# State-space layer of a four-layer network: input and output statistics move from VectorE to ScalarE

## The reference, cut to what matters

```python
u = x.reshape(Bsz, C, H * W).transpose(0, 2, 1)
fx = _layernorm(u, ln1_g, ln1_b)                # over the 384 channels
Bu = jnp.einsum('ph,blh->blp', B_bar, fx)       # 192 complex states
_, xs = jax.lax.associative_scan(binop, (lam_el, Bu), axis=1)
y = 2.0 * jnp.real(jnp.einsum('hp,blp->blh', Cc, xs)) + D * fx
y = jax.nn.gelu(y, approximate=False) + fx
fy = _layernorm(y, ln2_g, ln2_b)
z1, z2 = jnp.split(fy @ W_enc.T, 2, axis=-1)
y = (z1 * jax.nn.gelu(z2, approximate=False)) @ W_dec.T + fy
```

## Time and profile before

| what | us |
|---|---|
| median of three runs (lowest to highest) | 4251.5 (4245.55 to 4254.65) |
| the profiled execution, its own time | 4248.17 |
| its span in the trace | 4246.4 |
| state-space layer: first group norm to its last output store issued | 1891.5 to 2651.6 |
| VectorE busy, whole span | 3092.6 (73%) |
| TensorE busy, whole span | 3846.9 (91%) |
| ScalarE busy, whole span | 2300.1 (54%) |

### The profile page before, as it was taken

How to read it: one execution, slowest core, us unless ns; L and a number is a source line. 1 busy time by engine, 2 the same in 40 slices (tenths; PEclk the granted TensorE clock), 3 DMA queues, 4 the chain that set the end, 5 groups by cost and what they waited for, 6 DMA issues and landing times. The chain is left out here.

```text
span 4246.4 us, 54195 instructions
## 1 busy us (share of the span) xinstructions
PE 3846.9 (91%) x17373; PEld 2366.5 (56%) x17373; DVE 3092.6 (73%) x3183; ACT 2300.1 (54%) x3658; POOL 1402.0 (33%) x1142
## 2 busy tenths in 40 slices
PE   6999999999999999955899999465999999999999
PEld 5776868686867677722455555244444444444444
DVE  4767666676767675647989886356878888888878
ACT  1867767685858585834443442223544644644644
POOL 1857667575748485831211100221000000000000
PEclk8999999999999999977999999688999999999999
DMA  3333324242324332220121112775011010010010
GB/s 118 85 93 93 102 82 112 74 116 78 102 84 106 89 95 79 59 79 32 38 80 55 50 45 62 198 220 187 0 45 43 2 44 33 11 44 25 20 44 15
DMA packets 117836, 312.13 MB, mean 74 GB/s; under 512 B 48146, under 2 KB 49762, under 8 KB 108914
## 3 DMA queue, kind: packets, MB, share of 16 engines
q1 hardware_dynamic: 105650, 264.17, 20.7%
q0 software_dynamic: 10960, 37.38, 3.9%
q10 hardware_dynamic: 1008, 7.67, 0.5%
HBM read 203.12 MB, written 101.30 MB: 72 GB/s over the span
## 5 line engine op out<-in xcount | busy, mean ns | idle before, releaser
L417 POOL TENSOR_TENSOR probs_lo<-probs,probs_hi 128x512 fp32r<-128x512 f32 x848 | 1169.2, 1394 | 641.7 <-ACT probs L463 620.8
L530 DVE TENSOR_REDUCE maxima<-m_psum 128x1 fp32r<-128x1024 f32 x512 | 625.1, 1222 | 368.1 <-PE m_psum L706 367.4
L462 ACT ACTIVATE probs_hi<-s_psum 128x512 fp32r<-128x512 f32 x1024 | 613.3, 599 | 383.5 <-PE o_psum L735 221.8
L2510 PE MATMUL psum<-mixes,last_weights 128*128 128x512 f32 x1728 | 751.1, 592 | 0.0
L463 ACT ACTIVATE probs<-s_psum 128x512 f32<-128x512 f32 x1024 | 609.0, 595 | 0.0
L2510 PEld LDWEIGHTS psum<-mixes,last_weights 128*128 128x128 f32 x1728 | 327.5, 190 | 409.8 <-issue 409.8
L719 PE MATMUL s_psum<-q_all,k_hi 128*128 128x512 f32 x1024 | 430.8, 421 | 25.9 <-ACT probs L463 25.6
L735 PE MATMUL o_psum<-probs_lo,v 128*112 128x512 f32 x1024 | 412.1, 402 | 12.7 <-DVE probs_lo L610 6.5
L730 PE MATMUL o_psum<-probs_hi,v 128*112 128x512 f32 x1024 | 404.4, 395 | 0.0
L720 PE MATMUL s_psum<-q_all,k_lo 128*128 128x512 f32 x1024 | 404.3, 395 | 0.0
L2517 PE MATMUL psum<-xp,last_weights 128*128 128x512 f32 x864 | 381.9, 596 | 18.3 <-DVEq L2394 13.3
(11 more groups left out here) (338 smaller groups left out, 6240.3 us busy)
## 6 DMA issues: line engine op xcount, KB each, us to landing
xin<-x SPq DMA_DIRECT2D x17, 1536.0 KB, 6.8
xin<-in_x SPq DMA_DIRECT2D x16, 1536.0 KB, 7.3
k_hi<-k_rows_hi SPq DMA_DIRECT2D x128, 192.0 KB, 3.4
k_rows_hi<-stage_hi SPq DMA_DIRECT2D x48, 256.0 KB, 2.1
k_rows_lo<-stage_lo SPq DMA_DIRECT2D x48, 256.0 KB, 2.3
q_rows_hi<-stage_hi SPq DMA_DIRECT2D x48, 256.0 KB, 2.2
q_rows_lo<-stage_lo SPq DMA_DIRECT2D x48, 256.0 KB, 2.6
k_lo<-k_rows_lo SPq DMA_DIRECT2D x64, 192.0 KB, 4.4
```

What stands on the lines that cost most here:

```text
L417: pool.tensor_tensor(probs_lo[:, u % RING, :], probs[:, u % RING, :], as_f32(probs_hi[:, u % RING, :]), ALU.subtract).then_inc(pool_low.ne ...
L462: nc.scalar.activation(probs_hi[:, u % RING, :], s_psum[:, u % 2, :], ACT.Exp, scale=SCALE)
L530: nc.vector.tensor_reduce(maxima[:, g % 2, tile:tile + 1], source, AX.X, ALU.max, negate=True).then_inc(rows_max.next(), 1)
L2510: ins = nc.tensor.matmul(bank, conv_w[:, t, down, factor, m * P:(m + 1) * P], mixes[:, factor, t, down:down + S, :].rearrange("p a b -> p ...
```

## The change

Half-width output statistics and full-width input statistics are taken by ScalarE: `output_sums` runs an Identity and a Square over 128 x 1536 values with `accum_out`, for each half of a batch, and `input_sums` runs an Identity and a Square over each of the three 128 x 1024 tiles of batch i+3. What they write besides the sums goes to `first_sums`, which is not read. VectorE only reduces and scales the sums (`moments`, `out_moments`). ScalarE also writes the whole result of half 0 (`wholes(i, 0)`), between the two halves of `highs`. On ScalarE gate 2 now comes before `affine` of norm1, and the half-1 output sums of batch i-1 between gates 1 and 2; the input sums come after gate 5, the half-0 output sums after the second Gelu. On VectorE two of the late `outputs` of batch i-1 move ahead of `lows` half 0; the third stays, and `out_moments(i-1)` stands between gate 1 and `scale` of norm1. For the first three batches VectorE still takes the input statistics with `bn_stats`. TensorE waits for `y_hi` tile by tile.

```diff
-        out_stats = sb("out_stats", [P, 6, 6])
+        x_sums = sb("x_sums", [P, 2, CT])
+        out_sums = sb("out_sums", [P, 2, 2])
...
-        f_first_half, f_second_half = (signal(n, CT) for n in ("f_first_half", "f_second_half"))
+        f_made = signal("f_made", 2 * CT)
+        x_summed = signal("x_summed")
+        out_summed = signal("out_summed", 4)
@@ -1219,22 +1222,40 @@
-            def highs(i):
+            def highs(i, half):
                 if i > 0:
                     act.wait_ge(hidden.sem, hidden.at(4 * CT, i - 1))
-                for half in range(2):
-                    act.wait_ge(scaled2.sem, scaled2.at(half + 1, i))
-                    for t in range(CT):
-                        nc.scalar.activation(y_hi[:, t, cols(half)], y[:, t, cols(half)], ACT.Identity,
-                                             scale=rows["ln2_g"][:, t:t + 1], bias=rows["ln2_b"][:, t:t + 1]).then_inc(high_made.next(), 1)
-
...
+            def wholes(i, half):
+                if i >= 2 and half == 0:
                     act.wait_ge(stored, 16 * (i - 1))
                     act.wait_ge(out_measured.sem, out_measured.at(1, i - 2))
                 for t in range(CT):
-                    nc.scalar.activation(residuals[i % 2][:, t, cols(1)], y[:, t, cols(1)], ACT.Identity,
-                                         scale=rows["ln2_g"][:, t:t + 1], bias=rows["ln2_b"][:, t:t + 1]).then_inc(f_second_half.next(), 1)
+                    nc.scalar.activation(residuals[i % 2][:, t, cols(half)], y[:, t, cols(half)], ACT.Identity,
+                                         scale=rows["ln2_g"][:, t:t + 1], bias=rows["ln2_b"][:, t:t + 1]).then_inc(f_made.next(), 1)
+
+            def input_sums(i):
+                act.wait_ge(x_loaded, 16 * (i + 1))
+                for n in range(2 * CT):
+                    t, kind = n // 2, n % 2
+                    if n >= 2:
+                        act.wait_ge(x_summed.sem, x_summed.now() - 1)
+                    nc.scalar.activation(first_sums[:, 1 + kind, :], xin[:, t * T:(t + 1) * T], (ACT.Identity, ACT.Square)[kind],
+                                         accum_out=x_sums[:, kind, t:t + 1]).then_inc(x_summed.next(), 1)
+
+            def output_sums(i, half):
+                act.wait_ge(out_made.sem, out_made.at(CT * (half + 1), i))
+                for kind in range(2):
+                    if x_summed.count:
+                        act.wait_ge(x_summed.sem, x_summed.now())
+                    if out_summed.count:
+                        act.wait_ge(out_summed.sem, out_summed.now())
+                    nc.scalar.activation(first_sums[:, :, cols(half)], residuals[i % 2][:, :, cols(half)], (ACT.Identity, ACT.Square)[kind],
+                                         accum_out=out_sums[:, kind, half:half + 1]).then_inc(out_summed.next(), 1)
@@ -1265,16 +1286,21 @@
                 if batch(i):
                     inverses(norm2, varied2, inv_made2, i)
-                    highs(i)
+                    highs(i, 0)
+                    wholes(i, 0)
+                    highs(i, 1)
                 if batch(i + 2):
                     inverses(norm1, varied1, inv_made1, i + 2)
                 if batch(i):
                     gates(i, 0, 1)
-                    wholes(i)
+                    wholes(i, 1)
                     gates(i, 1, 2)
+                if batch(i - 1):
+                    output_sums(i - 1, 1)
+                if batch(i):
+                    gates(i, 2, 3)
                 if batch(i + 2):
@@ -1285,22 +1311,38 @@
                 if batch(i):
-                    gates(i, 2, 2 * CT)
+                    gates(i, 3, 2 * CT)
+                if batch(i) and batch(i + 3):
+                    input_sums(i + 3)
                 if batch(i + 1):
                     for n in range(2 * CT):
                         act.wait_ge(y_plain.sem, y_plain.at(n + 1, i + 1))
                         at = y[:, n % CT, cols(n // CT)]
                         nc.scalar.activation(at, at, ACT.Gelu).then_inc(y_gelu.next(), 1)
+                        if n == 1 and batch(i):
+                            output_sums(i, 0)
+                elif batch(i):
+                    output_sums(i, 0)
+                    output_sums(i, 1)
 
         def _(dve):
+            def early_moments(i):
+                dve.wait_ge(x_loaded, 16 * (i + 1))
+                gn.vector_moments(dve, xin[:, :], step, None, gn_moments)
 
             def moments(i):
-                gn.vector_total(dve, 2 * CT, step, None, gn_moments)
+                dve.wait_ge(x_summed.sem, 2 * CT * (i - 2))
+                nc.vector.tensor_reduce(gn.both[:, :], x_sums[:, :, :], AX.X, ALU.add).then_inc(step.next(), 1)
+                dve.wait_ge(step.sem, step.now())
+                nc.vector.tensor_scalar(gn.both[:, :], gn.both[:, :], 1.0 / (CT * T), None, ALU.mult).then_inc(gn_moments.next(), 1)
+
+            def out_moments(i):
+                out = moments_out[:, i, :]
+                dve.wait_ge(out_summed.sem, out_summed.at(4, i))
+                nc.vector.tensor_reduce(out, out_sums[:, :, :], AX.X, ALU.add).then_inc(step.next(), 1)
+                dve.wait_ge(step.sem, step.now())
+                nc.vector.tensor_scalar(out, out, 1.0 / (CT * T), None, ALU.mult).then_inc(out_measured.next(), 1)
...
             def lows(i, half):
                 whole = residuals[i % 2]
-                if half == 0:
-                    if i >= 2:
-                        dve.wait_ge(stored, 16 * (i - 1))
-                    dve.wait_ge(scaled2.sem, scaled2.at(1, i))
-                    for t in range(CT):
-                        nc.vector.tensor_scalar(whole[:, t, cols(0)], y[:, t, cols(0)], rows["ln2_g"][:, t:t + 1], rows["ln2_b"][:, t:t + 1],
-                                                ALU.mult, ALU.add).then_inc(f_first_half.next(), 1)
                 for t in range(CT):
                     nth = CT * half + t + 1
-                    if half == 0:
-                        dve.wait_ge(f_first_half.sem, f_first_half.at(t + 1, i))
-                    else:
-                        dve.wait_ge(f_second_half.sem, f_second_half.at(t + 1, i))
                     dve.wait_ge(high_made.sem, high_made.at(nth, i))
+                    dve.wait_ge(f_made.sem, f_made.at(nth, i))
                     nc.vector.tensor_tensor(y_lo[:, t, cols(half)], whole[:, t, cols(half)], as_f32(y_hi[:, t, cols(half)]),
@@ -1426,27 +1458,12 @@
             def outputs(i, first, end):
                 xres = residuals[i % 2]
-                for n in range(first, end + 1):
-                    if n < end:
-                        m, half = n % CT, n // CT
-                        if n == 0:
-                            dve.wait_ge(res_added, 16 * CT * (i + 1))
-                        dve.wait_ge(decoded.sem, decoded.at(n + 1, i))
-                        nc.vector.tensor_tensor(xres[:, m, cols(half)], xres[:, m, cols(half)], bank("dec", i, n), ALU.add).then_inc(out_made.next(), 1)
-                    if first == 0 and n < CT and batch(i + 3):
-                        measure(i + 3, n)
-                    if n > first:
-                        last = n - 1
-                        dve.wait_ge(out_made.sem, out_made.at(n, i))
-                        nc.vector.bn_stats(out_stats[:, last, :], xres[:, last % CT, cols(last // CT)]).then_inc(step.next(), 1)
-                if end < 2 * CT:
-                    return
-                out = moments_out[:, i, :]
-                dve.wait_ge(step.sem, step.now())
-                dve.sem_inc(gn.turn, 1)
-                nc.vector.bn_aggr(out, out_stats[:, :, :].rearrange("p a b -> p (a b)")).then_inc(step.next(), 1)
-                dve.wait_ge(step.sem, step.now())
-                nc.vector.scalar_tensor_tensor(out[:, 1:2], out[:, 0:1], out[:, 0:1], out[:, 1:2], ALU.mult, ALU.add).then_inc(out_measured.next(), 1)
+                for n in range(first, end):
+                    m, half = n % CT, n // CT
+                    if n == 0:
+                        dve.wait_ge(res_added, 16 * CT * (i + 1))
+                    dve.wait_ge(decoded.sem, decoded.at(n + 1, i))
+                    nc.vector.tensor_tensor(xres[:, m, cols(half)], xres[:, m, cols(half)], bank("dec", i, n), ALU.add).then_inc(out_made.next(), 1)
@@ -1461,11 +1478,8 @@
+                    if i >= 1 and batch(i + 2) and n == 1:
+                        moments(i + 2)
...
@@ -1493,23 +1507,25 @@
+                def scale_second():
+                    if here:
+                        scale(norm2, y, inv_made2, scaled2, i)
+                    if batch(i - 1):
+                        outputs(i - 1, EARLY, 2 * CT - 1)
+                    if here:
+                        lows(i, 0)
+
                 if i == -2:
...
                 if after:
                     turn_in(i + 1, 1, scale_second)
-                elif here:
+                else:
                     scale_second()
                 if batch(i - 1):
```

(17 more changed lines are left out.)

23 lines of the change are left out of this document (7 added, 16 removed).

## The result

| kernel | median us (runs) | ratio to before, with interval |
|---|---|---|
| before, beside the first runs of after | 4253.07 (4) | |
| after | 4226.86 (4) | 0.994 (0.9924 to 0.9955) |
| before, beside the second set | 4248.81 (21) | |
| after, second set | 4229.1 (5) | 0.9956 (0.9943 to 0.997) |
| before, beside the third set | 4249.72 (11) | |

The changed kernel is faster by 0.6% (0.45 to 0.76%). The forecast was 4238.5 with a range from 4228 to 4250: the sign is right, the gain is about 22 us instead of 13, and the first median lies 1.1 us under the range. Repeats of the same kernel later came out at 4229.1 and 4227.5.

A forecast was written before the change was run, and what follows sets the result against it. The bound was a ring of VectorE's 63.4 us and TensorE's 22.0 us. Periods won 14.0 + 1.2 + 1.2 = 16.4 us, less 3.3 for clock falls, gave 13: 4251.5 - 13 = 4238.5, range 4228 to 4250.

The forecast's parts named there:

- The ring: Period closes through TensorE's 22.0 us and VectorE's 63.4 us, `centre` to `turn_out`; only shortening the 63.4 shortens it.
- the covered parts: ScalarE's input sums (8.4 us), half-0 output sums (3.5 us) and layer-end sums were claimed to fit inside existing slack.
- step 2: VectorE from gate 0 to `scale` of norm1: waiting for half-1 output sums gives back everything won at gate 0.
- the old joining: VectorE's joining of late output statistics before gate 0, put at 0.7 us and used to price `out_moments`.
- two falls in five at the C product: TensorE's clock falls behind its new 1.9 us stall, each fall 1.6 us on the ring: 3.3 us off.
- 16.4 - 3.3 = 13.1: Five full periods 14.0, batch 0's and batch 6's periods 1.2 each, together 16.4, less 3.3 for clock falls.
- the sums are nearly free: Rival: `accum_out` on ScalarE costs nothing and no clock falls; 19 us gained, 4232.5; chance 0.14.
- The tables: Rival: Square makes ScalarE reload its table, 1.28 us a load; 2 us gained, 4249.5; chance 0.07.
- Slower by the wait: Rival: VectorE waits at `out_moments` for costly ScalarE sums; at 2.0 us extra each, 4261; chance 0.06.
- The clock falls at every C product: Rival: TensorE's clock falls after every new stall there; 8 us gained, 4243.5; chance 0.18.
- It doesn't do what it says, since TensorE is the ring: Rival: TensorE sets the period, so at most its 1.9 us stalls go; gain 5 to 10 us; no separate chance.
- The rule that the prediction set against the idea: Skill page sends simple adds and multiplies to VectorE; a whole takes 0.74 us on ScalarE, under 0.5 on VectorE.

The follow-up runs named there:

- order only: Kernel before with gate 2 early, two decoder sums ahead, late output statistics behind `turn_out`, all statistics and half 0's wholes on VectorE: 4224.57 us, ratio 0.994.
- gate 2 late: Changed kernel with gate 2 put back behind `affine` of norm1 on ScalarE, all else kept: 4248.28 us, ratio 1.0.
- a third sum: Changed kernel with half 1's output sums by Identity taken twice, one more accumulating activation: 4246.28 us, ratio 0.999.
- gate 2 early: Kernel before with one edit, gate 2 ahead of `affine` of norm1 on ScalarE: 4237.29 us, ratio 0.9977.

## Why the prediction was too small

**What held.** The ring: of VectorE's work only what lies between `centre` and `turn_out` counted, and nine of twelve `bn_stats` were worth nothing (six of them by the run with input statistics put back; with order only, all twelve are on VectorE behind `turn_out`, at the shortest period). Measured from `centre`:

| step | before | after | moved | predicted |
|---|---|---|---|---|
| gate 0 on VectorE | 34.15 | 32.67 | -1.48 | -1.45 |
| `scale` of norm1 | 39.34 | 38.67 | -0.67 | 0 |
| wait at gate 2 | 3.23 | 0 | gone | gone |
| wait at gate 3 | 0 | 0.43 | +0.43 | +0.4 |
| gate 3 | 48.80 | 45.32 | -3.48 | -2.8 |
| C product | 63.38 | 59.93 | -3.45 | -2.8 |

Gate 0 was waited for 2.68 us (said: 2 to 3), TensorE's encoder stall went, its new stall before the C product is 1.38 (said: 1.9), and the covered parts stayed covered: the input sums took 6.3 us (said: 8.4, with a slip in it, since two thirds of 1.48 is 0.99 and not 1.14) and left ScalarE 7.96 us idle before the first Gelu. The runs support the two pairs of cause and effect, too: with gate 2 late the wait of 3.22 is back and with it the time; where the late outputs stay behind the low parts, the stall of 1.90 stays.

**The step that failed first** is step 2, "`scale` starts at 2387.75, just where it did: everything won at gate 0 is given back". The term that was mis-sized is what `out_moments` costs. I took 0.7 for the reduce and scale, the price of the old joining, and the top of my bounds (0.4 and 0.7): from the start of the reduce to `scale` it is 2370.79 - 2370.52 = 0.27, below both. The two sums took 2370.49 - 2367.25 = 3.24, not 3.46, since half of each accumulator's read overlaps. So 0.43 + 0.22 = 0.65 us a period passed on to everything behind: 5 x 0.65 = 3.3 us. The old joining is two instructions as well (0.32 and 0.22 us in the trace of before), but the aggregate also waits for the last of the statistics and reads 36 columns; the new two take 0.16 and 0.17. So `scale` did start earlier, by 0.67, and not just where it did.

**The second** is the clock: "I take two falls in five at the C product, each 1.6 us on the ring: 3.3 us off". None fell. The gap came out at 1.38 us, half a microsecond below what I had argued from, as the work on the ring ended earlier by the same 0.65. The price of a fall was right (1.69 in the run with a third sum), the rate wasn't: it fell in none of the 15 gaps of 1.37 to 1.40 in three profiles of the changed kernel. It fell at all five of 1.90 in the kernel before, in two of five at 1.90 with gate 2 early, in three of five at 2.75 with gate 2 late, and at all five of 2.45 to 2.47 with a third sum. Within one kernel the five come at nearly the same distance, so they may not be five separate tries, and what decides stays open. The two in five was a guess, and so the 3.3 us that it took off the sum were one too.

The rest is small: the last period won 1.5 instead of 1.2, the first 1.3 instead of 1.2, in the profile at hand; in the third profile of the same kernel the first period is 84.3 and wins nothing. Together 16.4 - 3.3 = 13.1 becomes 17.3 + 1.3 + 1.5 = 20.1, against 20.2 in the trace. This is my rival "the sums are nearly free", 19 us, at 0.14. The measured gain of the layer, 20.2, taken off the median shown would be 4251.5 - 20.2 = 4231.3, inside the range; that the first median is lower still, under my edge of 4228, fits the scatter outside the layer, for which I had allowed 4 us from 4232.5. Part of it is the anchor: three runs of before gave 4251.5, the larger sets 4248.8 to 4249.9, and these less 20.2 are 4228.6 to 4229.7, beside the three medians of after, 4226.9 to 4229.1. The later medians, 20 and 22 us below theirs of before, straddle 20.2. The chances have a slip that changes nothing: 0.49 + 0.14 + 0.09 is 0.72, not 0.71.

**The rivals.** *The tables* is refuted: a Square runs at 2368.91 between two gates with no load near it, and loads stay two a period, 1.28 us each. The Trainium skill's page "ScalarE: Activation LUTs", section "Table sets: the hidden batching unit", doesn't list Square among the members of every set; here the Gelu set served it. *Slower by the wait* has its mechanism confirmed by the third sum and its price refuted: an accumulating activation costs 0.18 us over a plain one (1.66 from start to start against 1.48), where the rival's break-even was about 1.05. *The clock falls at every C product* is refuted at the gap that came, 1.38. *It doesn't do what it says, since TensorE is the ring*, is false of after, whose period shortens when VectorE's wait is moved; it is nearer to true at 80.8, 1.1 us further on, where two kernels with 70.8 and 78.0 us of VectorE work have the same period. The rule that the prediction set against the idea, simple work to VectorE, holds for the wholes of half 0 alone, and less by the length of an instruction than by what stood behind them in ScalarE's queue.

**What I did not see** is that my own ring told of a cheaper change. The 63.4 us held one wait of 3.23 us, caused by the place of one gate in ScalarE's queue, and one TensorE stall, caused by two additions behind low parts. Those two moves are 18.6 of the 20.2 us, and the work moved to ScalarE is the smaller part, at the wholes even a loss. What of the change is good is its order. Not tried: whether the 1.15 us before the decoder part, for `prod`, can be had by shortening or reordering VectorE's work ahead of it.

## What to carry to other kernels

Before moving work off an engine that looks full, walk the ring that closes the period and price the waits in it: a wait that stands there because of an order in another engine's queue is worth its length down to the next wait behind it (3.23 us less 0.43 here), while busy time outside the ring is worth nothing. A VectorE at 97% with the right order made a shorter period than one at 85% with a wait of 2.68 us in it. And where a sum gives several small terms that all hang on unseen instructions, work out once what the time would be if all of them were at their lower bound together, since they also set the size of the gap that bears on the clock.

## What the runs showed of the hardware

- An accumulating activation costs a second instruction of 0.19 us for the read of the accumulator. Back to back, six 1024-wide ones came 1.04 us apart, as long as each activation itself (1.04 to 1.05); two plain 1536-wide ones back to back take 2.86 us together, 0.1 less than twice 1.48, so the read costs some 0.1 there. Where the next one waits for the first's result it is 1.66 us from start to start at 1536 columns, against 1.48 for the activation.
- Gaps of one and the same length, 1.90 us, with the same waiter and releaser, made TensorE's granted clock fall in some periods and left it in others, in the kernel with gate 2 early; gaps of 2.75 with gate 2 late did so in three of five, while 2.45 did all five times and 1.38 never. A gap's length alone doesn't decide it. Nor does the fall come at one moment: in the kernel before the first microsecond behind the gap is granted 0.50 in full (2378.65 to 2379.65), with gate 2 early it is granted 1.00 (2450.05 to 2451.05) and the second one 0.51. A fall cost the period 1.6 to 1.7 us where TensorE had no time to spare behind it, and 0.4 at most with gate 2 late, where it had.
- A reduce of 128x4 and a scale of 128x2 on VectorE took 0.16 and 0.17 us, and from the start of the first to the start of what follows it was 0.27.
